# Attention with routed experts on one core: the experts' low parts and the rounding of q and k made on GpSimd, the bank copies spread anew

## The chip, the cores and the metric

The kernel runs on one core of a Trainium2 chip. The metric is the device time of one execution in microseconds (us). The engines of the core take their own instructions in order and wait for each other through semaphores: TensorE (PE, with its weight loads as PEld), VectorE (DVE), ScalarE (ACT), GpSimd (POOL), and the queue of SyncE (SP, in rows SPq), which issues transfers.

## What is computed

x has 4 x 1024 rows of 512 numbers in fp32. Each row is normalised; the result goes through causal attention (16 heads of 32, with a linear position bias) and through a layer of 8 experts of which each row uses two. Both are added to x.

```python
xn = _layernorm(x, axis=-1)
x = x + _L0_attn_ref(xn, Wq, bq, Wk, bk, Wv, bv, Wo, bo) + _L0_ffn_ref(xn, gate_w, w1, w2)
# attention, per batch b and head h
q, k, v = proj(Wq, bq), proj(Wk, bk), proj(Wv, bv)
scores = jnp.einsum('bhqd,bhkd->bhqk', q, k) / math.sqrt(D)
scores = jnp.where(causal, -jnp.inf, scores) + alibi_bias
out = jnp.einsum('bhqk,bhkd->bhqd', softmax(scores), v)
# experts
topw, sel = jax.lax.top_k(softmax(x @ gate_w.T), 2)      # weights normalised to sum 1
gate_up = jnp.einsum('th,eoh->eto', x, w1)
g, u = jnp.split(gate_up, 2, axis=-1)
out = combine(jnp.einsum('eti,ehi->eth', silu(g) * u, w2))
```

## The kernel before

Large products are made in fp16, with each fp32 factor split in two: a high part (rounded to fp16) and a low part (the rest, rounded again). A product is then three matmuls: high by high, high by low, low by high.

The attention is one long loop over 512 units `u`, each one tile of 128 queries of one head: 4 batches, 4 groups of 4 heads, 8 query tiles. For a unit, TensorE makes the scores (`score`, L1087), VectorE adds the bias and takes the row's extreme in one pass (`mx`, L1480), ScalarE makes the exponentials (`exp`, L1670), and four units later TensorE transposes them in fp32 (`tr`, L1098) into one of two transposition banks `T`. A copy `pt` out of the bank is made by ScalarE (L1684) or by VectorE (L1491). Then come the products with v (L1114), the scaling (`rsb`, `a32`) and on GpSimd the split of the result in two (`aT`, L1779 and L1780).

Between the units stand the steps of other work, one or two per unit: the normalisation of the next batch, the projections of the next group of heads, the output projection (`o`, L1137, and `y`, L1518) with a reload of x (`oload`, L942 on SP), to which GpSimd adds the output's bias (`xbo`, L1786), the routing, and the preparation of the experts' weights.

For projected q and k there is one fp32 tile `t32`. ScalarE scales the projection into it (`qk32`, L1660), VectorE rounds it to fp16 (`qkh`, L1461), GpSimd makes the low part (`qkl`, L1769), and only then is the tile free for the next `qk32`. After four of these, 12 transfers on the SP queue (`stack`, L932) spread the result over the partitions.

The experts' weights pass in 56 chunks, numbered from 0: 32 of 128x704 and 24 of 512 columns. For each, the SP queue loads the raw chunk (two buffers), ScalarE makes the high part (`wsh`, L1703), VectorE the low part (`wsl`, L1552), and the SP queue stores both (`wstore`, L960). High and low part lie in `hl`, of which there is one: `wsh` of a chunk waits until the store of the chunk before has landed. A chunk takes four units. Chunks 0 to 9 come in batch 1, 10 to 32 from the end of batch 1 to batch 2, 33 to 55 from the end of batch 2 on. After the attention comes the experts' part (from about 1180 us).

A planner, `plan()`, writes all steps in one list; every engine walks through it and takes its own steps, so that list sets the order on each engine. Only the engine of the copies `pt` (and of `xt`, in the normalisation) is chosen by a balance: `lighter()` keeps a running estimate of ScalarE's and VectorE's work, `load`, in which each step adds its cost in us, gives the copy to the one with less, and lets the other lag by 2.0 us at most.

```python
    def lighter(n):
        m = max(load.values())
        for e in load:
            load[e] = max(load[e], m - 2.0)
        en = "act" if load["act"] <= load["dve"] else "dve"
        load[en] += 0.19 + n / (1200 if en == "act" else 960)
        return en[0]
```

## Time and profile before

| | us |
|---|---|
| median of three runs | 1640.9 |
| lowest and highest | 1637.94 and 1645.32 |
| the profiled execution | 1637.66 |
| its span, first to last instruction | 1635.9 |

| engine | busy us | share of the span |
|---|---|---|
| TensorE | 1479.2 | 90% |
| VectorE | 1047.6 | 64% |
| ScalarE | 888.6 | 54% |
| GpSimd | 567.1 | 35% |

The share over the whole span mixes the attention and the experts' part, in which other engines matter. So the table is to be read together with stretches: the projections and normalisations fall at 475 to 540 and 760 to 850 us, the splitting of the experts' weights at 400 to 475, 540 to 760 and 850 to 1070 us. An idle time of an engine counts only if the end waits for it, and the row of an instruction says what ended the idle time ahead of it.

### The profile page before, as it was taken

Reading aid. Unit: us, or ns where it says so; the run is one execution under the profiler, and the core shown is the slowest. Engines: PE = TensorE matmul, PEld = TensorE weight load, DVE = VectorE, ACT = ScalarE, POOL = GpSimd, SP = SyncE. Lnnn points to the kernel's source line nnn. Section 1 sums busy time; section 2 is a strip of 40 time slices with the busy share of each in tenths; the row PEclk is TensorE's granted clock in tenths of the full one; section 3 lists DMA queues with packets and bytes.
Section 4 is the critical chain, followed back from the end, with each engine's and each line's share of the span. In section 5 each row is a group of like instructions: output and inputs, shape, how many; then the busy total and the mean of one; then the engine's idle time right before and its main releaser. Section 6 shows DMA issues by size and latency. Waiting matters only on the chain.

```text
span 1635.9 us, 35508 instructions
## 1 busy us (share of the span) xinstructions
PE 1479.2 (90%) x12763; PEld 889.9 (54%) x12763; DVE 1047.6 (64%) x2485; ACT 888.6 (54%) x2029; POOL 567.1 (35%) x595
## 2 busy tenths in 40 slices
PE   3799988998998899989799898999889999999995
PEld 1465555655555555655455466565356656566563
DVE  6688787666778767777878877777334333333331
ACT  4477776665777666676766565667312222222221
POOL 3111132121113222112311134231215777777775
PEclk9899999999999999999999899999989999999998
DMA  6244431433423243542324241324687888788783
GB/s 254 74 131 114 123 91 58 112 104 101 118 90 96 88 136 115 149 128 76 97 64 116 77 115 52 87 78 164 220 260 110 136 129 141 129 140 136 127 145 45
DMA packets 171350, 193.28 MB, mean 118 GB/s; under 512 B 87536, under 2 KB 121072, under 8 KB 171056
## 3 DMA queue, kind: packets, MB, share of 16 engines
q1 hardware_dynamic: 143760, 151.67, 34.3%
q0 software_dynamic: 26128, 37.24, 13.7%
q8 instruction: 110, 1.80, 0.5%
q10 hardware_dynamic: 1296, 2.11, 0.3%
q14 instruction: 56, 0.46, 0.1%
HBM read 93.45 MB, written 53.74 MB: 90 GB/s over the span
## 4 chain that ended last, share of the span: by engine, by line
PE 67%; DVE 11%; issue 7%; ACT 5%; DMA 4%; SPq 4%; POOL 2%; DVEq 0%; POOLq 0%; ACTq 0%
PE S L1175 15%; PE T L1098 11%; PE O L1114 7%; PE S L1055 5%; PE S L1087 5%; PE O L1206 4%; PE M L1206 4%; PE M L1055 4%; DVE arena L1480 4%; SPq L932 3%; PE S L1072 2%; PE M L1137 2%; PE M L1072 2%; ACT arena L1670 2%; DVE arena L1491 1%
## 5 line engine op out<-in xcount | busy, mean ns | idle before, releaser
L1480 DVE CUSTOM_DVE_ANT_0 arena<-S,cF,nsl 128x1024 f32<-128x1024 f32 (+7 forms) x512 | 413.2, 811 | 60.0 <-PE S L1087 56.9
L1098 PE MATMUL T<-cF,arena 128*128 128x128 f32 x2304 | 368.1, 281 | 77.4 <-ACT arena L1684 42.6
L1670 ACT ACTIVATE arena<-arena,mneg 128x1024 f32<-128x1024 f32 (+7 forms) x512 | 395.4, 772 | 47.8 <-DVE mneg L1480 46.8
L1684 ACT ACTIVATE arena<-T 128x512 f32<-128x512 f32 (+3 forms) x544 | 241.8, 457 | 276.3 <-PE T L1098 274.2
L1098 PEld LDWEIGHTS T<-cF,arena 128*128 128x128 f32 x2304 | 267.9, 142 | 179.2 <-ACT arena L1684 47.8
L1175 PE MATMUL S<-arena 128*128 x1704 | 270.4, 316 | 8.9 <-issue 8.9
L1823 POOL DMA_INDIRECT out<-arena x142 | 222.1, 1564 | 106.8 <-ACT arena L1730 53.7
L1491 DVE COPY arena<-T 128x512 f32<-128x512 f32 (+3 forms) x288 | 153.6, 536 | 138.8 <-PE T L1098 137.0
L1175 PEld LDWEIGHTS S<-arena 128*128 128x128 f16 x1704 | 167.9, 99 | 108.4 <-issue 10.3
L1114 PE MATMUL O<-arena 128*32 128x128 f32 (+1 forms) x3328 | 211.3, 330 | 8.3 <-DVE arena L1511 7.1
L1087 PE MATMUL S<-arena 96*128 96x512 f16 (+3 forms) x768 | 213.1, 332 | 3.8 <-DMA arena<-arena 2.5
L1769 POOL TENSOR_TENSOR arena<-arena 128x512 f16<-128x512 f32 x64 | 75.3, 1177 | 302.4 <-DVE arena L1461 302.4
L1605 DVE COPY arena<-T 128x512 f16<-128x512 f16 x71 | 30.1, 424 | 220.5 <-PE T L1190 193.1
L1714 ACT ACTIVATE arena<-S,sc 128x352 f32<-128x352 f32 x71 | 39.3, 553 | 204.0 <-PE S L1175 195.9
L1779 POOL CAST arena<-arena 128x256 f16<-128x256 f32 x64 | 25.7, 401 | 328.0 <-DVE arena L1511 328.0
L1114 PEld LDWEIGHTS O<-arena 128*32 128x32 f32 x3328 | 67.1, 108 | 130.0 <-issue 114.2
L1055 PE MATMUL S<-arena 128*128 128x512 f16 x420 | 109.5, 389 | 0.1
L1786 POOL TENSOR_TENSOR arena<-arena 128x512 f32<-128x512 f32 x32 | 42.2, 1328 | 170.2 <-DMA arena<-in_x 170.2
L1670 ACT ACTIVATION_READ_ACCUMULATOR arena<-arena,mneg 128x1 f32 x512 | 99.9, 195 | 0.0
L1722 ACT ACTIVATE arena<-arena 128x352 f16<-128x352 f32 x71 | 35.2, 496 | 109.4 <-DVE arena L1591 106.3
L1055 PE MATMUL M<-arena 128*128 128x512 f16 x348 | 89.1, 384 | 4.8 <-DVE arena L1406 4.8
L1810 POOL DMA_INDIRECT arena<-xn_d,tl x71 | 72.8, 1025 | 51.7 <-DMA arena<-arena 29.9
(187 smaller groups left out, 1822.3 us busy)
## 6 DMA issues: line engine op xcount, KB each, us to landing
arena<-arena SPq DMA_DIRECT2D x192, 128.0 KB, 2.4
arena<-in_w1T SPq DMA_DIRECT2D x64, 352.0 KB, 3.5
arena<-in_x SPq DMA_DIRECT2D x64, 256.0 KB, 3.4
w_d<-arena SPq DMA_DIRECT2D x32, 352.0 KB, 2.9
arena<-w_d SPq DMA_DIRECT2D x16, 704.0 KB, 7.2
arena<-in_w2T SPq DMA_DIRECT2D x32, 256.0 KB, 2.9
out<-arena SPq DMA_DIRECT2D x32, 256.0 KB, 3.2
xn_d<-arena SPq DMA_DIRECT2D x24, 256.0 KB, 2.0
```

Source lines behind the costliest of these rows:

```text
L1055: tp = pe.matmul(z[:, :], wqkv[:, w_, c, f:f + P], xnT[:, a, c, half * 512:half * 512 + 512], start=(third == 0 and c == 0), stop=(third = ...
L1087: tp = pe.matmul(z[:, n0:n1], stk[par][0:96, h, 0, j * P:(j + 1) * P], stk[par][0:96, h, 1, n0:n1], start=True, stop=True)
L1098: tp = pe.transpose(z[:, (c - c0) * P:(c - c0 + 1) * P], ring[u % 4][:, c * P:(c + 1) * P], idf)
L1114: tp = pe.matmul(OB[32 * x:32 * x + 32, f:f + n], V[par][:, kt, x * D:(x + 1) * D], flat[:, x, c * P:c * P + n], start=(kt == 0), stop=(kt ...
L1175: tp = pe.matmul(y[:, i * 512:i * 512 + I], xT[:, s % XDEEP, 4 * a + c, :], weights[:, bass.ds(reg[s] + (w_ * NX * W1N + c * 2 * I + i * I ...
L1206: tp = pe.matmul(z[:, :], aTm[0:n, v, 2 * c + a, :], weights[0:n, bass.ds(r2 + (2 * NX * W1N + w_ * NX * W2N + c * E), E)], start=(k == 0) ...
L1480: dve.tensor_tensor_reduce(ring[r][:, 0:w], SBK[o.bank["score", u]][:, 0:w], rel[:, S - w:S], nsl[:, hh:hh + 1], 3.0e38, ALU.add, ALU.min, ...
L1491: dve.tensor_copy(PT[k][:, h, to_:to_ + gap * (c1_ - c0_ - 1) + 1:gap, :], TB[o.bank["tr", u, i]][:, 0:n].rearrange("p (c n) -> p c n", n= ...
L1670: act.activation(ring[r][:, 0:w], ring[r][:, 0:w], ACT.Exp, bias=mneg[:, m:m + 1], scale=-1.0, accum_out=rs[:, k, c:c + 1]).then_inc(sems[ ...
L1684: act.activation(PT[k][:, h, to_:to_ + gap * (c1 - c0 - 1) + 1:gap, :], TB[o.bank["tr", u, i]][:, 0:n].rearrange("p (c n) -> p c n", n=P), ...
L1769: pool.tensor_tensor(st[:, 2 * qk + 1, lo:hi], t32[:, 0, :], st[:, 2 * qk, lo:hi], ALU.subtract).then_inc(sems["qkl"], 1)
L1823: pool.indirect_dma_start(out=halves, out_offset=bass.IndirectOffsetOnAxis(row[:, part, s:s + 1].bitcast(U32), 0), in_=yo[:, s % YDEEP, c0 ...
```

## The change

Three things are edited. The low part of the experts' weights, one instruction on VectorE, becomes two on GpSimd: the raw chunk is multiplied by its scale in place, and the high part is subtracted. The rounding of q and k (`qkh`) goes to GpSimd but for the first group of the first batch; it keeps all its waits. And both are taken out of VectorE's side of the balance, which spreads the copies anew: `pt` goes from 544 on ScalarE and 288 on VectorE to 466 and 366. Apart from the engine of these copies the list of steps is the same.

```diff
@@ plan
         def rest():
             add("qk32", b, g, qk, half)
             o.leave("M", key, ("qk32", b, g, qk, half))
             load["act"] += 0.7
-            load["dve"] += 0.4
...
-        add("qkh", b, g, qk, half)
+        add("qkh", b, g, qk, half, sem="qkhp" if b or g else "qkhd")
...
             add("wsl", i)
-            load["dve"] += 0.9
@@ vector
-            elif kind == "qkh":
+            elif kind == "qkh" and not (key[0] or key[1]):
...
-            elif kind == "wsl":
-                i, = key
-                n, rows = w_rows(i)
-                s = col(S1) if WCHUNK[i][1] < 4 else col(S2)
-                on.wait_ge(*at("wsh", i))
-                dve.scalar_tensor_tensor(hl[0:rows, 0, 1, 0:n], raw[0:rows, o.bank["wload", "split", i], 0:n], s[0:rows],
-                                         hl[0:rows, 0, 0, 0:n], ALU.mult, ALU.subtract).then_inc(sems["wsl"], 1)
@@ gpsimd
+            elif kind == "wsl":
+                i, = key
+                n, rows = w_rows(i)
+                s = col(S1) if WCHUNK[i][1] < 4 else col(S2)
+                on.wait_ge(*at("wsh", i))
+                w = raw[0:rows, o.bank["wload", "split", i], 0:n]
+                then(pool.tensor_scalar(w, w, s[0:rows], None, ALU.mult))
+                pool.tensor_tensor(hl[0:rows, 0, 1, 0:n], w, hl[0:rows, 0, 0, 0:n], ALU.subtract).then_inc(sems["wsl"], 1)
+            elif kind == "qkh" and (key[0] or key[1]):
+                b, g, qk, half = key
+                lo, hi = half * 512, half * 512 + 512
+                on.wait_ge(*at("qk32", *key))
+                gb, gg = (b, g - 1) if g else (b - 1, NG - 1)
+                for h in range(4):
+                    on.wait_ge(*at("stack", gb, gg, h))
+                pool.tensor_copy(st[:, 2 * qk, lo:hi], t32[:, 0, :]).then_inc(sems["qkhp"], 1)
```

GpSimd's order before, in batch 2 around chunk 17 (L1769 is the low part of q or k, L1786 the bias on the reloaded x, which waits for its load, L1779 and L1780 the split of the attention's result):

```order
L1769 TENSOR_TENSOR arena<-arena 128x512 [waits s_qkh]
L1786 TENSOR_TENSOR arena<-arena 128x512 [waits s_res0]
L1779 CAST arena<-arena 128x256 [waits s_a32]
L1780 TENSOR_TENSOR arena<-arena 128x256 [waits s_pstep]
L1769 TENSOR_TENSOR arena<-arena 128x512 [waits s_qkh]
```

The same place after the change. In it L1757 and L1758 are the new low part (of chunk 16, then of 17), L1766 the new rounding, L1771 what was L1769, L1788 what was L1786, L1781 and L1782 what were L1779 and L1780:

```order
L1757 TENSOR_SCALAR arena<-arena,sc 128x704 [waits s_wsh]
L1758 TENSOR_TENSOR arena<-arena 128x704 [waits s_pstep]
L1766 CAST arena<-arena 128x512 [waits s_stack02,s_stack01,s_stack03,s_stack00,s_qk32]
L1771 TENSOR_TENSOR arena<-arena 128x512 [waits s_qkhp]
L1788 TENSOR_TENSOR arena<-arena 128x512 [waits s_res0]
L1781 CAST arena<-arena 128x256 [waits s_a32]
L1782 TENSOR_TENSOR arena<-arena 128x256 [waits s_pstep]
L1757 TENSOR_SCALAR arena<-arena,sc 128x704 [waits s_wsh]
L1758 TENSOR_TENSOR arena<-arena 128x704 [waits s_pstep]
L1766 CAST arena<-arena 128x512 [waits s_qk32]
L1771 TENSOR_TENSOR arena<-arena 128x512 [waits s_qkhp]
```

The low part of chunk 17 stands behind the bias on the reloaded x and behind the split of the result, and the next rounding and low part of k behind it.

VectorE's order before, at the same place (L1480 is the bias and extreme of a unit, with a short second instruction each; L1552 the low part of chunk 17, L1461 the rounding, L1498 and L1503 the reciprocals of the row sums):

```order
L1552 SCALAR_TENSOR_TENSOR arena<-arena,sc 128x704 [waits s_wsh]
L1480 ISA arena,mneg<-S,cF,nsl 128x896 [waits s_score,s_tr]
L1480 ISA mneg 128x1
L1498 RECIPROCAL rs<-rs 128x8 [waits s_exp]
L1503 TENSOR_SCALAR arena<-rs,sc 128x256 [waits s_rt,s_dstep]
L1480 ISA arena,mneg<-S,cF,nsl 128x256 [waits s_score,s_tr]
L1480 ISA mneg 128x1
L1461 CAST arena<-arena 128x512 [waits s_qk32]
```

And after the change (L1473 is what was L1480, L1484 the copy out of a bank, L1491 and L1496 what were L1498 and L1503):

```order
L1484 COPY arena<-T 128x512 [waits s_tr]
L1473 ISA arena,mneg<-S,cF,nsl 128x896 [waits s_score,s_tr]
L1473 ISA mneg 128x1
L1484 COPY arena<-T 128x128 [waits s_tr]
L1491 RECIPROCAL rs<-rs 128x8 [waits s_exp]
L1496 TENSOR_SCALAR arena<-rs,sc 128x256 [waits s_rt,s_dstep]
L1473 ISA arena,mneg<-S,cF,nsl 128x256 [waits s_score]
```

The low part and the rounding are gone, and two copies out of the transposition banks stand there that ScalarE made before.

## Rows read from the trace of the kernel before

**Rows 1.** Windows, three stretches: start:end, length, busy us (count) by engine, clock, DMA.
```profile
core 0: us, PE busy (x) PEld busy (x) DVE busy (x) ACT busy (x) POOL busy (x), PEclk, DMA share, GB/s
400.00:475.00 75.00, 69.53 (x641) 40.74 (x643) 59.16 (x133) 55.53 (x128) 10.55 (x14) 0.98 0.43 126
540.00:760.00 220.00, 208.00 (x1946) 122.64 (x1939) 158.71 (x354) 149.94 (x348) 40.62 (x46) 0.98 0.41 121
850.00:1070.00 220.00, 201.54 (x1773) 124.62 (x1772) 176.25 (x481) 130.97 (x309) 60.59 (x58) 0.97 0.30 85
```
**Rows 2.** Groups by line: out<-in, count | busy us, mean ns | idle before, releaser.
```profile
L1098 PE MATMUL T<-cF,arena 128*128 128x128 f32 x2304 | 368.1, 281 | 77.4 <-ACT arena L1684 42.6 <-DVE arena L1491 32.1
L1684 ACT ACTIVATE arena<-T 128x512 f32<-128x512 f32 (+3 forms) x544 | 241.8, 457 | 276.3 <-PE T L1098 274.2
L1491 DVE COPY arena<-T 128x512 f32<-128x512 f32 (+3 forms) x288 | 153.6, 536 | 138.8 <-PE T L1098 137.0
L1769 POOL TENSOR_TENSOR arena<-arena 128x512 f16<-128x512 f32 x64 | 75.3, 1177 | 302.4 <-DVE arena L1461 302.4
L1552 DVE SCALAR_TENSOR_TENSOR arena<-arena,sc 128x704 f16<-128x704 f32 (+2 forms) x56 | 49.3, 880 | 11.4 <-ACT arena L1703 11.4
L1703 ACT ACTIVATE arena<-arena,sc 128x704 f16<-128x704 f32 (+2 forms) x56 | 45.2, 807 | 20.8 <-DMA w_d<-arena 20.8
L1461 DVE CAST arena<-arena 128x512 f16<-128x512 f32 x64 | 29.0, 452 | 7.0 <-ACT arena L1660 7.0
L1779 POOL CAST arena<-arena 128x256 f16<-128x256 f32 x64 | 25.7, 401 | 328.0 <-DVE arena L1511 328.0
```
**Rows 3.** Timeline, 601 to 606 us: start, us, engine, line, out<-in, [idle before <-releaser].
```profile
601.06 0.60 SPq L960 DMA_DIRECT2D w_d<-arena  x1
...
604.10 0.88 ACT L1703 ACTIVATE arena<-arena,sc 128x704 f16<-128x704 f32 x1 [4.09 <-DMA w_d<-arena]
...
605.01 0.95 DVE L1552 SCALAR_TENSOR_TENSOR arena<-arena,sc 128x704 f16<-128x704 f32 x1 [3.66 <-ACT arena L1703]
...
605.52 0.33 PE L1098 MATMUL T<-cF,arena 128*128 128x128 f32 x1 [2.83 <-ACT arena L1684]
```
**Rows 4.** First and last of the six store waits; sum of six windows around them.
```profile
452.09 0.88 ACT L1703 ACTIVATE arena<-arena,sc 128x704 f16<-128x704 f32 x1 [3.03 <-DMA w_d<-arena]
...
960.57 0.72 ACT L1703 ACTIVATE arena<-arena,sc 128x512 f16<-128x512 f32 x1 [2.52 <-DMA w_d<-arena]
...
sum 37.00, PE 29.23 PEld 20.16 DVE 22.05 ACT 16.72 POOL 4.25; mean PE 4.87 PEld 3.36 DVE 3.68 ACT 2.79 POOL 0.71
```
**Rows 5.** Chain of waits, one of eight such pieces: start, us, what.
```profile
625.20 0.85 DVE arena L1552
```
**Rows 6.** Timeline of VectorE: a rounding beside work of GpSimd.
```profile
652.53 1.50 DVE L1461 CAST arena<-arena 128x512 f16<-128x512 f32 x1
```
**Rows 7.** Timeline around the store of chunk 17.
```profile
626.09 0.52 SPq L960 DMA_DIRECT2D w_d<-arena  x1
...
628.11 1.55 POOL L1786 TENSOR_TENSOR arena<-arena 128x512 f32<-128x512 f32 x1 [8.39 <-DMA arena<-in_x]
...
629.66 0.88 ACT L1703 ACTIVATE arena<-arena,sc 128x704 f16<-128x704 f32 x1
...
630.08 0.67 POOL L1780 TENSOR_TENSOR arena<-arena 128x256 f16<-128x256 f32 x1
```
**Rows 8.** Timeline: GpSimd ahead of chunks 15, 38 and 40, and ScalarE's next high part.
```profile
608.95 1.37 POOL L1786 TENSOR_TENSOR arena<-arena 128x512 f32<-128x512 f32 x1 [12.34 <-DMA arena<-in_x]
...
612.79 0.88 ACT L1703 ACTIVATE arena<-arena,sc 128x704 f16<-128x704 f32 x1
...
887.64 1.28 POOL L1786 TENSOR_TENSOR arena<-arena 128x512 f32<-128x512 f32 x1 [11.73 <-DMA arena<-in_x]
...
890.43 0.71 ACT L1703 ACTIVATE arena<-arena,sc 128x512 f16<-128x512 f32 x1
...
906.62 0.67 POOL L1780 TENSOR_TENSOR arena<-arena 128x256 f16<-128x256 f32 x1
...
908.74 0.71 ACT L1703 ACTIVATE arena<-arena,sc 128x512 f16<-128x512 f32 x1
```

13 lines of the change are left out of this document (4 added, 9 removed).

## The prediction

> **What bounds the kernel now.** I read first the engines' busy time in stretches, then the costliest groups, then the waits one by one in the order of time. The change acts on the attention part alone, from about 90 to 1180 us, and mostly on the three stretches in which the experts' weights are split in two (400 to 475, 540 to 760, 850 to 1070 us, 515 us together). There TensorE is busy for 69.53 + 208.00 + 201.54 = 479.1 us, so it sits idle for 35.9 us; VectorE is busy for 394.1 us (77%), ScalarE for 336.4 us (65%), GpSimd for 111.8 us (22%) [rows 1]. TensorE is the bound and both helpers have slack on average; what can be won is the idle time of TensorE. Its largest idle time is ahead of the fp32 transpositions (77.4 us in the whole run), which wait until ScalarE or VectorE has emptied a transposition bank [rows 2].
>
> One wait is special. The high part of each chunk of weights (`wsh`, ScalarE) goes into the only buffer `hl`, so it waits until the store of the chunk before has landed: 20.8 us in 8 waits [rows 2]. The longest is 4.09 us at 604.10 us; VectorE then waited 3.66 us for ScalarE and TensorE 2.83 us [rows 3]. Six of the eight make up 20.4 us of it, the first of them 3.03 us, the last 2.52 us. In the six windows around them TensorE was idle for 37.0 - 29.2 = 7.8 us [rows 4]. So TensorE lost 38% of such a wait on average, and 2.83 of 4.09, or 69%, in the worst.
>
> **Part 1, the low part leaves VectorE.** `wsl` took 56 x 880 ns = 49.3 us there [rows 2]. On the chain of waits of the three stretches eight of its pieces stand, 0.86 us or less each, about 6.5 us together; one is at 625.20 us [rows 5]. That is what its removal can give directly, less what is next late behind each.
>
> **Part 2, the rounding of projected q and k leaves VectorE.** 60 of its 64 casts go: 60 x 452 ns = 27.1 us [rows 2]. About half lie in the three stretches. One of them took 1.50 us instead of 0.45 us, at 652.53 us, where GpSimd was working beside it [rows 6]. The Trainium skill, "SBUF — State Buffer", section "SBUF: two separate sides", says that VectorE in a two-port mode, or with two SBUF inputs, and GpSimd lock one shared port pair for a whole instruction; the long cast agrees with it. By that rule the edit also ends those collisions, worth about 1 us each, and the new GpSimd work makes a few others; I count neither.
>
> **Part 3, the copies out of the transposition banks.** The order of the steps is the same but for the engine of the copy: ScalarE makes 466 copies for 544, VectorE 366 for 288. ScalarE gives up 78 x 457 ns = 35.6 us and VectorE takes 78 x 536 ns = 41.8 us [rows 2]. VectorE's balance is 49.3 + 27.1 - 41.8 = 34.6 us less, so each of the two is relieved by about 35 us of the 1090 us, nearly all in the three stretches: there VectorE falls from 77% to about 70% and ScalarE from 65% to about 59%.
>
> **The gain.** Of the 35.9 us of idle time in the stretches 7.8 us belong to the store waits, which this relief doesn't shorten. The other 28.1 us are the most that can be had. The eight pieces on the chain give perhaps half of their 6.5 us, the banks that are emptied earlier about as much again, and the rest of the attention, where only the casts and a few copies change, 1 to 2 us. I take 8 us, between 2 and 18.
>
> **Part 4, what GpSimd now has to do.** A low part is two instructions that wait for each other. The subtraction of 128x704: a subtraction of 128x512 took 1177 ns [rows 2], in proportion 1.62 us; some of it is a fixed part, so I take 1.5. The multiplication has one input: the nearest row is a cast of 128x256 in 401 ns [rows 2], in proportion 1.10 us, and I take 0.9. So 2.4 us for 704 columns (1.6 if neither grew with the width, 3.2 if the multiplication were as slow as the subtraction) and 1.8 us for 512 columns (the same two in proportion), for 0.88 us on average on VectorE. The cast of q or k, 512 columns, is at most 0.8 us. All together 32 x 2.4 + 24 x 1.8 + 60 x 0.7 = 162 us, on an engine that was busy 22% there: no bound by its sum. The Trainium skill, "GPSIMD Engine Reference", section "Engine selection", speaks against such a move: elementwise work belongs on VectorE, GpSimd being about 2 times slower with two inputs. The rows bear it out, with 2.4 us for 0.88 where one instruction becomes two; by the page's factor alone a low part would take 1.8 us, and the first two waits below would be 0.6 us shorter each.
>
> Its place in the queue matters more. GpSimd takes its work in order, and `xbo`, the bias added to a reloaded tile of x, waits there for that load. `wsl` now stands behind it, and behind `wsl` the store on the SP queue, and behind the store the next `wsh` on ScalarE, with all exponentials and copies after it. Of the chunks, counted from 0, most are not hurt: GpSimd starts at once where VectorE came to it later, in its turn, or the 12 stacking transfers keep the SP queue busy past the end of the low part anyway. Four have an `xbo` just ahead. A store takes 3.0 us from its issue to the start of `wsh` (601.06 to 604.10) [rows 3].
> - Chunk 17: `xbo` runs from 628.11 to 629.66, the two `aT` instructions end at 630.75, so `wsl` would end at 633.15 and the store, issued at 626.09 before, would be in at 636.2. ScalarE came to chunk 18 at 629.66: it would wait 6.5 us [rows 7].
> - Chunk 15: `xbo` ends at 610.3, `wsl` at 612.7, store in at 615.7, ScalarE there at 612.79: 2.9 us [rows 8].
> - Chunk 38: `xbo` ends at 888.9, `wsl` at 890.7, store in at 893.7, ScalarE there at 890.43: 3.3 us [rows 8].
> - Chunk 40: `aT` ends at 907.3, `wsl` at 909.1, store in at 912.1, ScalarE there at 908.74: 3.4 us [rows 8].
>
> That is 16.1 us of new waits of ScalarE. A handful of others (behind the bursts of stacking transfers, where chunks follow each other closely) grow by 0.5 to 1.3 us, which TensorE hardly feels, since it covered 2.1 us of each wait in rows 4 with work in hand, (20.4 - 7.8) / 6. TensorE's share of 16.1 us is 6.1 us at 38% and 11.1 us at 69%. I take 7 us, between 3 and 18 (all of the waits, and 3.2 us for a low part, which adds 0.8 us to each wait).
>
> The rounding is nearly free there: q and k's low part already ran on GpSimd behind it, so the pair only grows by some 0.3 us and saves VectorE's queue. The stores and loads keep their places on SP; the experts' weights are read back behind the last store, which comes before the attention's end, so the experts' part (from 1180 us on) is moved but not changed.
>
> **The sum.** 1637.7 us of the profiled execution (span 1635.9) - 8 + 7 = 1636.7 us. The median of the three runs is 3.2 us above the profiled one, at 1640.9, so the forecast is 1640 us.
>
> **Rivals.**
> A. *The relief is worth more.* Every unit of scores passes VectorE, ScalarE and a bank in turn, and the modelled ends of matmuls hide further gaps that don't count as idle. If 18 of the 28 us go and the store waits cost 3, the time is 1641 - 15 = 1626 us. For it: the 77.4 us ahead of the transpositions. Against it: TensorE is busy for 93% of the stretches already.
> B. *GpSimd's queue becomes the wait* (slower). The low part, blocked behind `xbo` by the reload of x, stops ScalarE through the store and the single buffer. Price: all 16.1 us, 0.8 us more for each of the four, a few of the small ones, together 18 to 22 us, less a gain of 3: 1641 + 17 = 1658 us. It decides as soon as TensorE loses over three quarters of each wait. For it: the 69% at 604 us; against it: the 38% of all six.
> C. *The balance does nothing*: a copy waits for its transposition either way (ScalarE's copies had 276.3 us of such idle time ahead of them, VectorE's 138.8 us [rows 2]), so moving copies wins nothing and the result is the casts' and low parts' 3 us against 7 us lost: 1645 us. It lies inside my own case.
>
> **How the numbers follow.** A difference under 0.5% (8 us) can't be told from none here. My case, within 8 us of 1641 with C in it: 0.55. A: 0.26. B: 0.19. The predicted time is 1640 us. The range runs from 1628 to 1655 us: it holds my case and the nearer halves of A and B. Faster by over 0.5% 0.26, within 0.55, slower 0.19.
>
> **What would show it.** The low part's two instructions at 0.9 and 1.5 us. ScalarE's wait ahead of `wsh` for the store: from 20.8 to about 37 us, with a new one of 5 to 7 us in the second pass of projections (near 636 us). VectorE's busy time down by some 35 us, ScalarE's by about the same, GpSimd's up by 150 to 165. TensorE's idle time ahead of the transpositions, 77.4 us, about unchanged in sum: less at the banks, more at the new waits. The forecast is wrong if no such wait stands near 636 us (then A), or if TensorE idles for nearly all of each (then B).

## The result, and the profile after

The changed kernel takes 1683.4 us (median of four executions, 1679.4 to 1686.2), the kernel before 1640.1 us (four, 1637.9 to 1645.3): a ratio of 1.026, with an interval from 1.023 to 1.029. It is slower by 43 us. The forecast was 1640 us with a range up to 1655 us, so the result lies well above it, on the side of rival B and beyond its price.

The table of engines and the chain that ended last, page of the kernel after (span 1683.4 us, before 1635.9):

```profile
PE 1498.2 (89%) x12763; PEld 893.7 (53%) x12763; DVE 1012.2 (60%) x2446; ACT 861.2 (51%) x1952; POOL 781.2 (46%) x767
...
PE 58%; DVE 9%; DMA 9%; POOL 8%; issue 8%; SPq 4%; ACT 4%; DVEq 0%; POOLq 0%; ACTq 0%
```

VectorE and ScalarE are relieved, by 35.4 and 27.4 us. But GpSimd has 214 us more, and TensorE, with the same number of matmuls, 19.0 us more. GpSimd holds 8% of the chain where it held 2%, and TensorE 58% where it held 67%.

The costliest groups by line of the kernel after (out<-in, count | busy us, mean ns | idle before, releaser). They answer to the rows in [rows 2]: L1096 to L1098, L1670 to L1684, L1484 to L1491, L1689 to L1703; L1757 and L1758 are the low part, L1766 the rounding.

```profile
L1096 PE MATMUL T<-cF,arena 128*128 128x128 f32 x2304 | 371.4, 282 | 102.3 <-ACT arena L1670 57.8 <-DVE arena L1484 39.4 <-ACT arena L1656 1.2
L1670 ACT ACTIVATE arena<-T 128x512 f32<-128x512 f32 (+3 forms) x466 | 210.5, 460 | 276.0 <-PE T L1096 274.1
L1484 DVE COPY arena<-T 128x512 f32<-128x512 f32 (+3 forms) x366 | 189.8, 528 | 198.3 <-PE T L1096 196.8
L1689 ACT ACTIVATE arena<-arena,sc 128x704 f16<-128x704 f32 (+2 forms) x56 | 45.3, 810 | 83.6 <-DMA w_d<-arena 83.4
L1766 POOL CAST arena<-arena 128x512 f16<-128x512 f32 x60 | 38.7, 644 | 103.6 <-ACT arena L1646 103.6
```

The one number that tells the story is 83.4 us: ScalarE waits that long ahead of the high part of a chunk (`wsh`) until the store of the chunk before has landed. It was 20.8 us in 8 waits; the list of waits of the kernel after (engine, line, waited for: us in total, times, longest) has

```profile
ACT arena L1689 <- DMA w_d<-arena: 83.4, 27, 8.1
```

The low part itself, groups of the kernel after with the shapes kept apart:

```profile
L1757 POOL TENSOR_SCALAR arena<-arena,sc 128x704 f32<-128x704 f32 x32 | 65.5, 2046 | 72.1 <-ACT arena L1689 72.1
L1758 POOL TENSOR_TENSOR arena<-arena 128x704 f16<-128x704 f32 x32 | 48.8, 1525 | 2.7
L1757 POOL TENSOR_SCALAR arena<-arena,sc 128x512 f32<-128x512 f32 x16 | 25.1, 1569 | 14.5 <-ACT arena L1689 14.4
```

The subtraction of 704 columns takes 1525 ns, as forecast (1.5 us). The multiplication, with one input less, takes 2046 ns: it is the slower of the two. A low part is 3.57 us, not 2.4.

Where this bites is seen in the chain of waits of the kernel after, around chunk 17 (start, us, what; [rows 7] of before is the same place):

```profile
632.29 2.68 DMA out<-arena
...
634.99 2.70 DMA arena<-in_x
...
637.75 1.27 POOL arena L1788
...
639.44 0.67 POOL arena L1782
640.11 2.03 POOL arena L1757
...
642.22 1.53 POOL arena L1758
...
643.77 2.85 DMA w_d<-arena
...
646.71 0.88 ACT arena L1689
```

Read from the top: an output tile is stored, so that its place is free; x is reloaded into it; GpSimd adds the bias to it (`xbo`, L1788), for which its queue had stood still 8.76 us; the split of the result (`aT`) and the low part follow; the store waits for the low part; and ScalarE waits for the store. The timeline of ScalarE at the end of it, and again one turn later (start, us, engine, line, out<-in, [idle before <-releaser]):

```profile
646.71 0.88 ACT L1689 ACTIVATE arena<-arena,sc 128x704 f16<-128x704 f32 x1 [7.35 <-DMA w_d<-arena]
...
692.67 0.88 ACT L1689 ACTIVATE arena<-arena,sc 128x704 f16<-128x704 f32 x1 [8.14 <-DMA w_d<-arena]
```

The first of these was 0 before. The second, ahead of chunk 22, was 3.39 us before already, since the store of chunk 21 stands behind a burst of twelve stacking transfers. SyncE's timeline in the kernel after shows what was added:

```profile
675.47 0.52 SPq L958 DMA_DIRECT2D w_d<-arena  x1
...
681.39 0.33 SPq L940 DMA_DIRECT2D arena<-in_x  x1
681.87 7.74 SPq L930 DMA_DIRECT2D arena<-arena  x12
689.66 0.60 SPq L958 DMA_DIRECT2D w_d<-arena  x1
```

The queue stands at the store of chunk 20 until that low part is done (675.44, again behind an `xbo` that waited 8.84 us for its load). The output's store, the next reload (which waits for that store to land, 681.37) and the burst all come behind it, and the store of chunk 21 last, at 689.66. A late low part delays the transfers behind it, these delay the next reload, and that the next low part.

Where the time goes, by the start of the bias-and-extreme instruction of single units on VectorE (us):

| unit | 208 | 256 | 288 | 336 | 368 | 400 | 511 |
|---|---|---|---|---|---|---|---|
| before | 500.8 | 599.7 | 676.0 | 778.4 | 842.4 | 927.6 | 1164.0 |
| after | 505.3 | 605.1 | 700.6 | 808.6 | 874.1 | 972.2 | 1210.4 |
| loss so far | 4.5 | 5.4 | 24.6 | 30.2 | 31.7 | 44.6 | 46.4 |

Most of it, 32 us, is lost between units 256 and 288 (19 us, chunks 15 to 22) and between 368 and 400 (13 us, chunks 34 to 41), and only 1 us in the experts' part. The windows of [rows 1] in the kernel after (start:end, length, busy us (count) by engine, granted clock, DMA):

```profile
400.00:475.00 75.00, 67.19 (x593) 38.71 (x592) 50.32 (x118) 48.05 (x116) 43.26 (x36) 0.93 0.36 108
540.00:760.00 220.00, 192.07 (x1773) 113.33 (x1777) 129.36 (x308) 126.45 (x292) 113.56 (x94) 0.95 0.38 110
850.00:1070.00 220.00, 189.81 (x1671) 113.18 (x1668) 161.97 (x453) 110.62 (x261) 112.21 (x101) 0.95 0.28 79
```

TensorE does 4037 matmuls in the three windows where it did 4360 (they are the same times, not the same units), although VectorE and ScalarE have less to do: VectorE is down to 342 of 515 us. GpSimd's busy time went from 112 to 269 us, still only 52%. No helper is full; what is full is a ring.

One stretch is different. Between units 368 and 400 the new waits of ScalarE for the store are 6.7 us, and 12.9 us are lost. TensorE's idle time ahead of the transpositions, in these 32 units before and after:

```profile
L1098 PE MATMUL T<-cF,arena 128*128 128x128 f32 x144 | 23.1, 283 | 10.9 <-DVE arena L1491 7.4 <-ACT arena L1684 3.4
L1096 PE MATMUL T<-cF,arena 128*128 128x128 f32 x144 | 23.2, 281 | 20.6 <-DVE arena L1484 17.5 <-ACT arena L1670 3.0
```

Here it is VectorE's copies that TensorE waits for, not ScalarE's: the new balance gives VectorE 29 of the 52 copies out of the banks in these units, where it had 19.

### The profile page after: what moved, and what is told of

It reads as the page before. It is cut to its first block, busy times and chain, and to the rows that moved or that the text cites. A ratio compares the mean times of both kernels' runs of the same rounds, so it can differ in the third digit from the quotient of the medians.

```text
span 1683.4 us, 35540 instructions
## 1 busy us (share of the span) xinstructions
PE 1498.2 (89%) x12763; PEld 893.7 (53%) x12763; DVE 1012.2 (60%) x2446; ACT 861.2 (51%) x1952; POOL 781.2 (46%) x767
## 4 chain that ended last, share of the span: by engine, by line
PE 58%; DVE 9%; DMA 9%; POOL 8%; issue 8%; SPq 4%; ACT 4%; DVEq 0%; POOLq 0%; ACTq 0%
PE S L1173 15%; PE T L1096 9%; PE O L1112 6%; PE S L1053 4%; PE S L1085 4%; PE M L1204 4%; PE O L1204 4%; PE M L1053 4%; SPq L930 3%; DMA out<-arena 3%; DMA w_d<-arena 3%; DVE arena L1473 3%; POOL arena L1757 2%; PE S L1070 2%; DVE arena L1484 2%
## 5 line engine op out<-in xcount | busy, mean ns | idle before, releaser
L1096 PE MATMUL T<-cF,arena 128*128 128x128 f32 x2304 | 371.4, 282 | 102.3 <-ACT arena L1670 57.8
L1473 DVE CUSTOM_DVE_ANT_0 arena<-S,cF,nsl 128x1024 f32<-128x1024 f32 (+7 forms) x512 | 413.3, 811 | 76.3 <-PE S L1085 73.5
L1096 PEld LDWEIGHTS T<-cF,arena 128*128 128x128 f32 x2304 | 268.5, 143 | 207.7 <-ACT arena L1670 52.3
L1670 ACT ACTIVATE arena<-T 128x512 f32<-128x512 f32 (+3 forms) x466 | 210.5, 460 | 276.0 <-PE T L1096 274.1
L1484 DVE COPY arena<-T 128x512 f32<-128x512 f32 (+3 forms) x366 | 189.8, 528 | 198.3 <-PE T L1096 196.8
L1112 PE MATMUL O<-arena 128*32 128x128 f32 (+1 forms) x3328 | 215.9, 336 | 7.2 <-DVE arena L1504 6.3
L1757 POOL TENSOR_SCALAR arena<-arena,sc 128x704 f32<-128x704 f32 (+2 forms) x56 | 103.2, 1843 | 93.9 <-ACT arena L1689 93.8
L1781 POOL CAST arena<-arena 128x256 f16<-128x256 f32 x64 | 26.3, 411 | 250.2 <-DVE arena L1504 250.2
L1788 POOL TENSOR_TENSOR arena<-arena 128x512 f32<-128x512 f32 x32 | 40.7, 1282 | 165.1 <-DMA arena<-in_x 165.1
L1053 PE MATMUL S<-arena 128*128 128x512 f16 x420 | 112.9, 398 | 0.0
```

The source lines that it names most:

```text
L1053: tp = pe.matmul(z[:, :], wqkv[:, w_, c, f:f + P], xnT[:, a, c, half * 512:half * 512 + 512], start=(third == 0 and c == 0), stop=(third = ...
L1096: tp = pe.transpose(z[:, (c - c0) * P:(c - c0 + 1) * P], ring[u % 4][:, c * P:(c + 1) * P], idf)
L1112: tp = pe.matmul(OB[32 * x:32 * x + 32, f:f + n], V[par][:, kt, x * D:(x + 1) * D], flat[:, x, c * P:c * P + n], start=(kt == 0), stop=(kt ...
L1473: dve.tensor_tensor_reduce(ring[r][:, 0:w], SBK[o.bank["score", u]][:, 0:w], rel[:, S - w:S], nsl[:, hh:hh + 1], 3.0e38, ALU.add, ALU.min, ...
L1484: dve.tensor_copy(PT[k][:, h, to_:to_ + gap * (c1_ - c0_ - 1) + 1:gap, :], TB[o.bank["tr", u, i]][:, 0:n].rearrange("p (c n) -> p c n", n= ...
L1670: act.activation(PT[k][:, h, to_:to_ + gap * (c1 - c0 - 1) + 1:gap, :], TB[o.bank["tr", u, i]][:, 0:n].rearrange("p (c n) -> p c n", n=P), ...
```

## The experiments

**Theory.** The loss is the low part on GpSimd, and of that its length in the ring `wsh` (0.88 us), low part, store (3.0 us), `wsh` through the single buffer `hl`. A chunk has about 8.5 us (four units; the median from one `wsh` to the next is 8.6 us before). With 0.88 + 3.57 + 0.2 + 3.0, about 7.6 us, there is about 1 us to spare, which any rounding (1.8 us with its low part), `aT` (1.1 us) or reload eats up. **Rivals:** the rounding on GpSimd does it; the new spread of copies does it; or, as rival B had it, the queue standing behind the reload, whatever the length; or GpSimd's longer busy time makes VectorE's instructions longer.

The trace of the kernel after shows the ring itself. Where one waiting `wsh` follows another without a break, from start to start it takes 7.54 to 7.60 us (chunks 3 to 4, 6 to 9, 26 to 28, 29 to 32). In `scale_tt`, whose low part is 0.69 us shorter, the least such turn is 6.80 us, and in `no_mult`, 2.05 us shorter, 5.39 us. Before the change eight turns of the chunks of 704 columns were shorter than 7.54 us, 5.68 to 7.29 us: they follow a long turn, and with them the chunks caught up. A ring of 7.6 us can't do that. The average room of 1 us hides that a delay is hardly made up any more.

The two traces speak against the last rival. VectorE's large groups did not get longer: the bias and extreme of 1024 columns takes 1276 ns before and after, a copy of 384 columns 554 ns, and the 64 scalings of 128x256 fell from 581 to 442 ns. The one group that grew, eight instructions of 128x1024 with two inputs, from 1274 to 1558 ns, adds 2.3 us in all.

### Which part: low part, rounding or copies

`low_back`: the low part back on VectorE, with its 0.9 us in the balance; rounding and balance of the rounding as after the change.

```diff
@@ plan
             add("wsl", i)
+            load["dve"] += 0.9
@@ gpsimd
-            elif kind == "wsl":      # moved to vector(), as before the change
```

> The changed kernel with the experts' low part back on VectorE, one instruction, and its 0.9 us back in the balance; the rounding of q and k stays on GpSimd. Theory of the store chain (the low part takes 2.05 + 1.53 us on GpSimd and holds back the store, the store the next high part on ScalarE, and so TensorE): all of the loss goes, 1632 to 1645 us, ScalarE's waits for the store back at about 20 us from 83. Rival, the rounding on GpSimd or the copies do the harm: over 1655 us.

`round_back`: the rounding alone back on VectorE, with its 0.4 us in the balance.

```diff
@@ plan
             load["act"] += 0.7
+            load["dve"] += 0.4
-        add("qkh", b, g, qk, half, sem="qkhp" if b or g else "qkhd")
+        add("qkh", b, g, qk, half)
@@ gpsimd
-            elif kind == "qkh" and (key[0] or key[1]):      # moved to vector()
```

> The changed kernel with the rounding of q and k back on VectorE and its 0.4 us back in the balance; the low part of the weights stays on GpSimd. Theory of the store chain: most of the loss stays, 1670 to 1685 us, since only 0.6 us per rounding leaves GpSimd's queue; ScalarE's waits for the store 70 to 80 us. Rival, the rounding behind a reload on GpSimd is the cause: under 1655 us.

`copies_only`: the kernel before with both costs taken out of the balance and no work moved.

```diff
@@ plan, kernel before
             load["act"] += 0.7
-            load["dve"] += 0.4
...
             add("wsl", i)
-            load["dve"] += 0.9
```

> The kernel before with the changed spread of the copies alone: low part and rounding stay on VectorE but are missing in its side of the balance, so VectorE gets 78 copies more on top of them, some 42 us of work. Theory that both helpers have slack and only waits count: within 5 us of the kernel before, 1635 to 1645 us. Rival, VectorE (77% busy in those stretches, 83% then) becomes a bound: over 1650 us.

`round_only`: the kernel before with the rounding on GpSimd and both costs still in the balance (as `low_back`, with the 0.4 us too).

```diff
@@ plan, against low_back
             load["act"] += 0.7
+            load["dve"] += 0.4
```

> The kernel before with the rounding of q and k on GpSimd and nothing else: the balance and so the spread of the copies are as before. low_back, which has the rounding's 0.4 us out of the balance as well, is 0.35% faster than the kernel before. If the 27 us less on VectorE are what gives it: the same, 1630 to 1635 us. If the new spread of the copies is what gives it: 1637 to 1640 us.

The ratios are against executions of the kernel before that were taken beside each kernel (medians 1637.4 to 1638.9 us).

| kernel | median us (runs) | against before | waits of ScalarE for the store |
|---|---|---|---|
| low_back | 1633.0 (10) | 0.9965 [0.994, 0.999] | 11.2 us |
| round_back | 1681.8 (4) | 1.0271 [1.022, 1.032] | 81.1 us |
| copies_only | 1654.1 (4) | 1.0093 [1.007, 1.012] | 19.0 us |
| round_only | 1632.5 (12) | 0.9964 [0.995, 0.998] | 11.2 us |

The group of `wsh` in `low_back`:

```profile
L1697 ACT ACTIVATE arena<-arena,sc 128x704 f16<-128x704 f32 (+2 forms) x56 | 45.1, 806 | 11.2 <-DMA w_d<-arena 11.2
```

So the loss comes with the low part: without it the kernel is even 5 to 6 us faster than before, and without the rounding it is as slow as the changed one. The rounding on GpSimd is a gain of 0.36% by itself, small, but with an interval that stays below 1. The spread that comes with it is worth nothing over the whole kernel (`low_back` and `round_only` are the same), but it is not the changed kernel's: `pt` is 508 on ScalarE and 324 on VectorE in `low_back`, 544 and 288 in `round_only`, 466 and 366 after the change. Where no work leaves VectorE the whole shift to 466 and 366 costs 15 us, against the 5 us at most that were expected: in `copies_only` VectorE is busy for 413 of the 515 us of the three windows and the idle time ahead of the transpositions grows, now mostly waiting for VectorE:

```profile
L1096 PE MATMUL T<-cF,arena 128*128 128x128 f32 x2304 | 367.5, 280 | 88.0 <-DVE arena L1489 53.7 <-ACT arena L1682 31.1
```

Between units 368 and 400 the spread shows in every kernel. They take 83.7 to 85.2 us with the old one, 89.4 and 91.1 us in `low_back_late` and `low_back`, and with the changed kernel's 91.7 (`no_mult_late`, see below), 93.1 (`no_mult`), 93.5 (`copies_only`) and 98.1 us (after). So, as far as these kernels tell, some 6 to 8 of the 13 us lost there go with the copies. `low_back` makes up its part elsewhere. Whether the changed kernel does can't be told: none was run with the low part on GpSimd and the copies as before.

### Length of the low part

`no_mult`: no multiplication; the low part is the subtraction alone, at the same place in the queue.

```diff
@@ gpsimd
                 w = raw[0:rows, o.bank["wload", "split", i], 0:n]
-                then(pool.tensor_scalar(w, w, s[0:rows], None, ALU.mult))
```

> The changed kernel without GpSimd's multiplication of the raw chunk by its scale, so the low parts of the experts' weights are made from unscaled numbers (that work is left out): the low part takes 1.53 us on GpSimd and not 3.65. Theory of the store chain: about what was forecast blind for a low part of 1.6 us, ScalarE's waits 25 to 40 us and a time of 1637 to 1650 us. Rival, the order of GpSimd's queue alone decides (a reload of x ahead of the low part, whatever the low part takes): over 1660 us.

`scale_tt`: the multiplication as an instruction with two inputs, of which the second is the scale's column repeated.

```diff
-                then(pool.tensor_scalar(w, w, s[0:rows], None, ALU.mult))
+                then(pool.tensor_tensor(w, w, s[0:rows].to_broadcast([rows, n]), ALU.mult))
```

> The changed kernel with the multiplication by the scale as a two-input instruction (the scale's column repeated over the row) in place of the one with a scalar from memory. The one with a scalar took 2.05 us for 704 columns, the two-input subtraction 1.53 us. If the two-input form takes 1.53 us here too, the low part falls to 3.1 us, and by the line through no_mult (1.53 us, 30.4 us of waits, 1644 us) and the changed kernel (3.65 us, 83.4 us, 1683 us) the waits are 68 us and the time 1672 us. Rival, reading a repeated column costs as much as the scalar: 1680 us and no change.

`imm_mult`: the factor is a constant of the instruction and not a column in memory.

```diff
-                then(pool.tensor_scalar(w, w, s[0:rows], None, ALU.mult))
+                then(pool.tensor_scalar(w, w, 1.5, None, ALU.mult))
```

> The changed kernel with the multiplication on GpSimd by a constant in the instruction, not by a scalar of each partition from memory (so the low parts are made from wrongly scaled numbers). It asks what the 2.05 us of the 704-column multiplication are. If the scalar from memory is what costs: near 0.8 us, and a time near 1655 us. If the one-input instruction on fp32 is slow by itself: 2.0 us and the time of the changed kernel.

`split_store`: the store of a chunk is cut in two, the high part leaves as soon as `wsh` is done; `wsh` of the next chunk then waits for that store and for the low part instruction, no longer for the low part's store.

```diff
@@ plan
             yield
+            add("whstore", i, sem="wdh", inc=16)
             add("wsl", i)
@@ scalar, ahead of wsh
-                    on.wait_ge(*at("wstore", i - 1))
+                    on.wait_ge(*at("whstore", i - 1))
+                    on.wait_ge(*at("wsl", i - 1))
@@ gpsimd, ahead of wsl
                 on.wait_ge(*at("wsh", i))
+                if i:
+                    on.wait_ge(*at("wstore", i - 1))
@@ sync
+                sp.dma_start((w1_d if c < 4 else w2_d)[:, 0, f:f + n], hl[:, 0, 0, 0:n]).then_inc(sems["wdh"], 16)
...
-                sp.dma_start((w1_d if c < 4 else w2_d)[:, :, f:f + n], hl[:, 0, :, 0:n]).then_inc(sems["wd"], 16)
+                sp.dma_start((w1_d if c < 4 else w2_d)[:, 1, f:f + n], hl[:, 0, 1, 0:n]).then_inc(sems["wd"], 16)
```

> The changed kernel with the store of a chunk cut in two: the high part is stored as soon as ScalarE has made it, the low part behind GpSimd. The next high part waits for the high part's store and for GpSimd's low part, but no longer for the 3.0 us store behind it; the next low part waits for the low part's store. All work of GpSimd and the copies are as in the changed kernel. Theory of the store chain: ScalarE's waits ahead of the high part fall from 83 us by 3.0 us for each of the 27, to 15 to 35 us, and the time to 1645 to 1660 us. Rival, GpSimd's longer busy time slows VectorE through their common port, or the copies on VectorE do the harm: no more than 5 us won, over 1675 us.

| kernel | median us (runs) | against before | low part, 704 columns | idle ahead of wsh |
|---|---|---|---|---|
| after | 1683.4 (4) | 1.0257 | 2.05 + 1.53 us | 83.4 us in 27 |
| imm_mult | 1678.9 (1) | one run | 1.97 + 1.5 us | 82.9 us in 29 |
| scale_tt | 1669.6 (4) | 1.0175 [1.015, 1.020] | 1.36 + 1.5 us | 64.0 us in 24 |
| split_store | 1656.5 (4) | 1.0124 [1.008, 1.017] | 2.05 + 1.5 us | 39.8 us |
| no_mult | 1644.3 (10) | 1.0046 [1.003, 1.006] | 1.5 us | 30.4 us in 15 |

The multiplication of 704 columns in `scale_tt` and in `imm_mult` (groups, shapes apart), and `wsh` in `no_mult`:

```profile
L1757 POOL TENSOR_TENSOR arena<-arena,sc 128x704 f32<-128x704 f32 x32 | 43.5, 1360 | 74.2 <-ACT arena L1689 74.2
```
```profile
L1757 POOL TENSOR_SCALAR arena<-arena 128x704 f32<-128x704 f32 x32 | 63.1, 1973 | 71.9 <-ACT arena L1689 71.9
```
```profile
L1689 ACT ACTIVATE arena<-arena,sc 128x704 f16<-128x704 f32 (+2 forms) x56 | 45.2, 807 | 30.4 <-DMA w_d<-arena 30.4
```

The time follows the low part's length. Taking 2.05 us off the low part of a chunk that has about 1 us to spare saves 39 us; 0.69 us off saves 14. The column in memory is not what makes the multiplication slow (1973 ns with a constant); the instruction `tensor_scalar` is, and the same product as `tensor_tensor`, also in place, takes 1360 ns. And cutting the ring at the store, with the low part as long as in the changed kernel and all of GpSimd's work kept, saves 27 us. The 39.8 us of waits that are left there are more than the 15 to 35 expected; they are put down to GpSimd (15.6), issue (12.3) and the store (11.9).

### The reload ahead of it

`no_xbo`: the addition of the output's bias to x is left out, so nothing on GpSimd waits for a reload; `y` waits for the load instead.

```diff
@@ plan
-        add("xbo", b, i)
@@ gpsimd
-            elif kind == "xbo":
-                ...
-                pool.tensor_tensor(buf, buf, bob[:, :], ALU.add).then_inc(sems["xbo"], 1)
```

> The changed kernel without the addition of the output's bias to the reloaded x on GpSimd (that work is left out; the step that adds the projection waits for the load itself), so no low part stands behind the reload of x any more. Blind it was forecast that the waits behind the reload are nearly all of the harm. Theory of the blocked queue: ScalarE's waits for the store fall from 83 us to 25 us or less and the time to under 1650 us. Rival, the length of the low part, 3.65 us against a slack of some 5 us per chunk, makes most of them by itself: waits of 45 to 60 us remain and the time is 1655 to 1670 us.

`late_xbo`: all work is kept, and `xbo` stands about five units later in the list, just ahead of the projection that needs it or of the next store of output.

```diff
@@ plan, o_load
         add("oload", b, i, sem=f"res{out_slot(b, i)}", inc=16)
-        add("xbo", b, i)
@@ plan, o_steps
+        due = list(range(n))
         for i in range(8):
...
+            while due and due[0] <= i:
+                add("xbo", b, due.pop(0))
             yield from proj_o(b, i)
             yield
+            if due:
+                add("xbo", b, due.pop(0))
             o_store(b, i)
             if i + n < 8:
                 o_load(b, i + n)
+                due.append(i + n)
```

> The changed kernel, all its work kept, with the bias on the reloaded x moved some five units later in the list of steps, to just ahead of the store of the next tile, where its load has landed; GpSimd no longer stands at it. Theory of the ring (reload of x, bias, low part, store of the low part, and behind that on the SP queue the next store and reload of x): time near that of no_xbo, 1645 to 1655 us, with waits of ScalarE for the store of 55 to 70 us, none above 6 us. Rival, no_xbo was faster because work was left out: 1670 us or more.

`no_xbo` takes 1647.4 us (5 runs; 1.0055 [1.004, 1.007]) and `late_xbo` 1649.2 us (9; 1.0063 [1.004, 1.008]). `wsh` in `late_xbo`:

```profile
L1694 ACT ACTIVATE arena<-arena,sc 128x704 f16<-128x704 f32 (+2 forms) x56 | 45.3, 809 | 60.0 <-DMA w_d<-arena 60.0
```

The two agree, so it is the place of the instruction and not its 1.3 us. In `no_xbo` the waits are 61.4 us; the time is the one that the blocked queue foretold, the waits are those of its rival, the low part's length. At first sight 34 us hang on the reload. But the waits for the store fall only from 83.4 to 60.0 us, so part of these 34 us must come from somewhere else. To tell it, the same edit was made where the low part is short or on VectorE.

### The reload moved in the other kernels

The same edit to `o_load` and `o_steps`, applied to `low_back` (`low_back_late`), to the kernel before (`before_late`), to `no_mult` (`no_mult_late`) and to `round_only` (`round_late`); and `repaired`, the changed kernel with `late_xbo`, `scale_tt` and `split_store` together:

```diff
@@ all five: the edits of late_xbo, and
-    low_back_late: nothing else against low_back
-    before_late:   nothing else against the kernel before
-    no_mult_late:  nothing else against no_mult
-    round_late:    nothing else against round_only
-    repaired:      scale_tt and split_store, against the changed kernel
```

> The kernel low_back (the low part on VectorE, the rounding on GpSimd, the copies spread for that) with the bias on the reloaded x moved later as in late_xbo. There nothing but the rounding and q's and k's low part stands behind the reload, with ScalarE's waits for the store at 11 us. Theory of the ring: no more than 3 us to win, 1629 to 1635 us. Rival, GpSimd standing at the reload still costs through q and k: 1625 us or less.

> The kernel before with the bias on the reloaded x moved later, nothing else. low_back_late has shown that this alone wins 18 us with the low part on VectorE; 10 us of it fall between units 144 and 160, where in the kernel before GpSimd's maximum of the experts' weights stood behind a reload and VectorE waited 7.6 us for it. If so, the gain is there in the kernel before too: 1617 to 1625 us, and only the rest of late_xbo's 34 us belongs to the ring of the change. If the gain of the later bias needs the change: 1635 us or more.

> late_xbo without GpSimd's multiplication (that work is left out): low part of 1.53 us and no reload ahead of it. With late_xbo (3.65 us, 1649 us) it gives the price of the low part's length when nothing else stands in GpSimd's queue. Theory of the store chain: waits of ScalarE 20 us or less, no loss left, 1615 to 1625 us. Rival, the copies or GpSimd's mere presence cost: 1635 us or more.

> round_only (rounding on GpSimd, balance and copies as before) with the bias moved later. If round_only's and the later bias's gains add: 1612 to 1618 us, the same as low_back_late within 3 us, so the copies' spread is worth nothing there.

> The changed kernel with the three repairs together: the bias on the reloaded x later, the scale by the two-input instruction (1.36 us for 2.05), and the store cut in two. GpSimd does all the work it got. Theory: ScalarE's waits fall to 10 us or less, the loss is gone and the relief of the two helpers shows, 1628 to 1640 us. Rival, GpSimd's work costs in some other way too (the common port, q and k's low part behind it): 1645 us or more.

| | xbo at its old place, us | xbo late, us |
|---|---|---|
| kernel before | 1638 | 1623.5 (before_late, 0.9918 [0.990, 0.994]) |
| rounding on GpSimd, copies as before (round_only) | 1632.5 | 1615.4 (round_late, 0.9866 [0.984, 0.989]) |
| rounding on GpSimd, copies half way to the new spread (low_back) | 1633.0 | 1614.6 (low_back_late, 0.9852 [0.983, 0.988]) |
| low part on GpSimd too, 1.53 us (no_mult) | 1644.3 | 1614.1 (no_mult_late, 0.9853 [0.983, 0.988]) |
| low part on GpSimd too, 3.57 us (after) | 1683.4 | 1649.2 (late_xbo) |

`repaired` comes to 1620.5 us (4 runs; 0.9898 [0.987, 0.993]); its low part takes 1.23 + 1.37 us on average, and 16.1 us of idle time are left ahead of `wsh`. It is 29 us under `late_xbo`, but 6 us above `low_back_late`: on VectorE the low part still stands better.

`low_back_late` was expected at 1629 to 1635 us, `no_mult_late` at 1615 to 1625 us and `repaired` at 1628 to 1640 us: all three came out below. The first miss showed that the later `xbo` helps also where no low part stands behind it. The reason is one more instruction in GpSimd's queue. It computes a maximum over all partitions (`wgmax`), for which VectorE waits at the start of the weights' preparation. GpSimd's timeline in the kernel before:

```profile
375.66 1.27 POOL L1786 TENSOR_TENSOR arena<-arena 128x512 f32<-128x512 f32 x1 [3.87 <-DMA arena<-in_x]
382.71 0.37 POOL L1764 PARTITION_ALL_REDUCE sc<-sc  x1 [5.78 <-issue]
```

The bias waits 3.87 us for its reload, and the maximum begins 5.78 us behind it. In `before_late` the idle time ahead of the maximum is as long, but it lies where nobody waits, since its input from VectorE is there only at 380.06:

```profile
373.60 1.27 POOL L1791 TENSOR_TENSOR arena<-arena 128x512 f32<-128x512 f32 x1 [0.35 <-DMA arena<-in_x]
380.58 0.37 POOL L1769 PARTITION_ALL_REDUCE sc<-sc  x1 [5.71 <-DVE sc L1534]
```

The wait of VectorE for it, in the list of waits of the kernel before and of `before_late`:

```profile
DVE sc L1226 <- POOL sc L1764: 7.6, 1, 7.6
```
```profile
DVE sc L1231 <- POOL sc L1769: 0.2, 1, 0.2
```

From unit 144 to unit 160 the kernel before takes 44.9 us and `before_late` 35.8. Of the 16.0 us by which `before_late` is ahead at unit 511 that is 9.1; 5.9 are gained in the last 15 units, 6.2 in between, and 5.2 lost before unit 144. Those other parts were not traced to single waits.

**What follows.** Against the kernel with the low part on VectorE (`low_back`, `low_back_late`), the low part on GpSimd costs 50.4 us with the old place of `xbo` and 34.6 us with the late one; a short low part (1.53 us) costs 11.3 us and nothing (-0.5). So the 45 us between the changed kernel (1683.4) and the kernel before (some 1638 us beside the experiments) divide in this way: about 35 us are the low part by itself, about 16 us the reload ahead of it, less 5 us that the rounding gains. That the 35 us are the low part's length, and not its being on GpSimd, is shown by the short one, which costs nothing there. That all of its cost passes through the store is not shown: between units 368 and 400 `late_xbo` is 6.9 us slower than `no_mult_late`, with only 0.5 us more of waits for the store. Both the theory and rival B hold a part, and length is the larger. The rounding holds none, and over the whole kernel no loss by the copies is seen: `no_mult_late`, with the full new spread, is level with `low_back_late` and `round_late`. The fastest kernels that do all the work are `low_back_late`, at 1614.6 us, 1.5% under the kernel before, and `round_late` beside it; their low part stands on VectorE, so the half of the change that was kept is the rounding.

The `wsh` of `low_back_late`, and that of `no_mult_late`, where the low part is on GpSimd and no store is waited for either:

```profile
L1702 ACT ACTIVATE arena<-arena,sc 128x704 f16<-128x704 f32 (+2 forms) x56 | 45.1, 805 | 12.0 <-DMA w_d<-arena 12.0
```
```profile
L1694 ACT ACTIVATE arena<-arena,sc 128x704 f16<-128x704 f32 (+2 forms) x56 | 45.2, 808 | 14.2 <-DMA w_d<-arena 14.2
```

## Why the prediction was wrong, step by step

**Right: the mechanism and its places.** The four waits that part 4 worked out are all in the timeline of ScalarE after the change: behind chunk 15 4.26 us (2.9 forecast), behind 17 7.35 (6.5), behind 38 4.65 (3.3), behind 40 3.18 (3.4). Their sum is 19.4 us against 16.1. The chain `xbo`, low part, store, `wsh` is the one that rival B names.

**Right: the relief.** VectorE fell by 35.4 us (34.6 said). The subtraction took 1.5 us and the rounding 0.64 us. A gain near 8 us is there once nothing waits: `no_mult_late` is 9.4 us under `before_late`. But that kernel leaves the multiplication out, and 8.1 of it is already in `round_late`; taking the low part off VectorE adds little over the scatter of the runs, and `repaired`, which does all the work, is only 3 us under `before_late`. So the term came out near its size by luck and was wrong in its division: the casts carry it, not the eight pieces of `wsl` on the chain; what took their place there was not traced. Half of rival C holds: the new balance of the copies won nothing (`low_back` against `round_only`, `low_back_late` against `round_late`). ScalarE fell by 27.4 us, where 35.6 was said, and GpSimd rose by 214 us where 150 to 165 was said: the multiplications took 103.2 us where the sum had some 45.

**Wrong, the first step: the price of the multiplication.** It was carried over from a cast of 256 columns, fp32 to fp16, 401 ns, and taken at 0.9 us. The row was the wrong one: another operation, another output type, and a third of the width. The cast of 512 columns takes 644 ns in the changed kernel and the multiplication of 512 columns 1569 ns. The upper bound was wrong too: "as slow as the subtraction" was put at the end of the range as if one input could not cost more than two, and it does, 2046 against 1525 ns. So the low part was 3.57 us with 3.2 as the worst case. The Trainium skill, "GPSIMD Engine Reference", section "Engine selection", puts GpSimd at about twice VectorE's time for an instruction with two inputs and calls one with a single input roughly line-rate. The trace does not bear out the second part: the multiplication, with one input, is the slower of the two. Together one VectorE instruction of 0.95 us [rows 3] became 3.57 us for the same 704 columns, 3.8 times as long. The page's advice, taken as a reason against such a move, pointed the right way, and its factor covered about half of the price.

**Wrong, the second step: "most are not hurt".** The other waits were called a handful of 0.5 to 1.3 us. They were 64 us in 23, where 20.8 us in 8 stood before: 43 us of new waiting. This rested on walking through the chunks with the times of before, each by itself. But a chunk has about 8.5 us, and 7.6 us of them are a ring which holds one buffer. When one turn is late by more than that, the next starts late as well, and with it SyncE's queue, in which the output's store, the reload and the twelve stacking transfers stand behind the late store (675 to 690 us). With a low part of 1.53 us the ring is about 5.5 us long (0.88 + 1.53 + 0.1 + 3.0); all waits are then 30.4 us in 15 and the time is 1644 us. A low part of 2.4 us, as forecast, lies between that kernel and `scale_tt` (2.9 us, 1670 us), so a kernel with the forecast's price would have been slower than 1644 us too; none was run.

**Wrong, the third step: what TensorE loses of a wait.** 38% was read from its idle time in six windows. In whole kernels that differ only in the length of the multiplication the span moved by 39.5 us for 53.0 us of waits (after against `no_mult`), 26.8 for 33.6 (`scale_tt` against `no_mult`) and 34.0 for 45.8 (`late_xbo` against `no_mult_late`): 75%, 80% and 74%. They are averages: in the last pair, units 160 to 208 and 288 to 336 lost about half of their new waits, 256 to 288 nearly all, and 368 to 400 more than they had. Idle time missed half of the loss. Read as in the prediction, in windows from the start of each wait until 1.6 us behind the start of `wsh`, TensorE's share after the change is still 39% (32.5 of 82.6 us, 25 waits). So the reading was right, and what failed is taking idle time for the whole loss. After the change TensorE is idle 28.5 us more, but busy 19.0 us more too, for the same 12763 matmuls: one of 128x512 took 398 ns where it had taken 389, at a mean granted clock of 0.965 for 0.976 (0.93, 0.95 and 0.95 in the three windows, where it had been 0.98, 0.98 and 0.97; the levels behind such a mean are 1.2 and 2.4 GHz). By that ratio alone 1479.2 us become 1496, which is nearly all of the 19. Rival B set its point of decision at three quarters of each wait; measured by the span, that is what came.

With 83.4 - 20.8 = 62.6 us of new waits in place of 16.1, and three quarters of them lost where 7 of 16.1 us were taken (44%), the span grew by 47.5 us where the sum had lost 7 and gained 8 (before any gain, 75 to 80% of 62.6 us would be 47 to 50 us). The waits were 3.9 times as long and TensorE's share 1.7 times as large, and the two multiply.

## What to carry to other kernels

An instruction that moves to another engine is priced by a row of that engine with the same operation, width and types; where no such row exists, the upper bound must not be taken from a row that only seems costlier, and the case is worth a measurement of its own. A path through a single buffer is to be added up as a ring, with what can stand ahead of each of its instructions, and held against the time of one turn: with 3 us to spare work on it could move freely (`no_mult_late`), if nothing ahead of it waited for a transfer; with some 1.7 us (`scale_tt`) it still cost 31 us, and with 1 us 45 us, both with `xbo` at its old place. The average turn is not enough: what counts are the short turns behind a long one, for the ring can't be walked faster than its length. And an instruction that waits for a transfer belongs, in an in-order queue, where the transfer has long landed: moving `xbo` by five units gave 14 to 18 us in the kernels where nobody had suspected it.

## What the runs showed of the hardware

- On GpSimd a multiplication fp32 to fp32 in place with one tensor input takes 2046 ns for 128x704 and 1569 ns for 128x512, with a constant for the factor 1973 ns; the form with two inputs, one of them a repeated column, takes 1360 ns for 128x704, and a cast of 128x512 to fp16 644 ns. The kind of instruction matters more than the number of inputs.
- A maximum over the partitions on GpSimd started 5.6 to 5.8 us behind the instruction ahead of it in every kernel but one, both where its input had long been there (before) and where it came 5.2 us behind that instruction (`before_late`). In `no_xbo` the input came 8.2 us behind, and the maximum started 0.14 us after it. So the time runs from the instruction ahead, and not from the input. If that instruction waits for a transfer, these microseconds come on top.
- TensorE's granted clock in the three windows was 0.93, 0.95 and 0.95 after the change, with its many short stops, and 1.00, 1.00 and 0.97 in `no_mult_late`, which has few. So a stop can cost more than its idle time. It is no fixed rule: `round_back`, with 81 us of waits for the store, has 1.00 in the first window.
- With 214 us more of work on GpSimd, VectorE's large groups kept their times (1276 ns before and after for 1024 columns of bias and extreme). Where GpSimd made only the rounding, VectorE's low part of 704 columns grew a little, from 958 ns before to 1030 ns in `round_late`.
